# Masks' stage of a graph attention layer: three tiles of sixteen take a mask of outer neighbours from VectorE, and denominators are inverted in a dense form reached by transfers

## What is computed

```
# x is layer-normed
seq = (x @ W_seq).reshape(N, H, DH)                     # N=2048, H=16, DH=32
score1, score2 = einsum('nhd,d->hn', seq, a1), einsum('nhd,d->hn', seq, a2)
scores = leaky_relu(score1[:, :, None] + score2[:, None, :], 0.2)
scores = scores + (1.0 - adj)[None, :, :] * MASK_VAL    # adj is 0 or 1
attn = softmax(scores, axis=-1)
hidden = einsum('hij,jhd->ihd', attn, seq)
```

## Time and profile before

| | us |
|---|---|
| median of three runs | 2346.68 (2344.52 to 2347.96) |
| the profiled execution | 2353.32 |
| its span | 2351.6 |
| masks' stage, first mask to last multiplication | 124.7 to 736.1 |
| PE, DVE, ACT busy over the span | 2117.2, 1557.5, 1090.1 |

### The profile page before, as it was taken

The page is one execution under the profiler, slowest core; times in us unless marked ns, Lnnn a source line. Parts: engine busy times, 40 slices in busy tenths (PEclk is TensorE's granted clock), DMA queues, the critical chain, the costliest instruction groups (busy, mean ns, idle before and its releaser), DMA issues. The chain is left out here.

```text
span 2351.6 us, 43031 instructions
## 1 busy us (share of the span) xinstructions
PE 2117.2 (90%) x18260; PEld 1238.6 (53%) x18260; DVE 1557.5 (66%) x2507; ACT 1090.1 (46%) x1071; POOL 552.0 (23%) x413
## 2 busy tenths in 40 slices
PE   6799999999996899969999998999992599999997
PEld 3444444444443344434444444444461488888886
DVE  7768888888885766747777778776336544444442
ACT  5667888888882233313344444444431222222221
POOL 0000000000001112333454555545521222222211
PEclk9899999999998999958999999999976699999999
DMA  7421211212114111353113031011030444444431
GB/s 253 142 62 42 72 52 62 75 39 76 49 47 156 64 50 72 136 124 76 29 28 82 19 80 29 23 37 46 23 135 36 152 117 117 117 117 113 113 66 23
DMA packets 81711, 185.27 MB, mean 79 GB/s; under 512 B 8785, under 2 KB 18001, under 8 KB 75985
## 3 DMA queue, kind: packets, MB, share of 16 engines
q1 hardware_dynamic: 72560, 161.56, 21.0%
q0 software_dynamic: 8960, 20.98, 4.8%
HBM read 137.81 MB, written 40.37 MB: 76 GB/s over the span
## 5 line engine op out<-in xcount | busy, mean ns | idle before, releaser
L450 ACT ACTIVATE m_step<-m_ub,gat_bias 128x2048 bf16<-128x2048 f32 x256 | 494.3, 1994 | 119.7 <-DVE m_mask L527 106.2
L1266 DVE TENSOR_REDUCE t_rm<-t_m 128x1 f32<-128x512 f32 (+3 forms) x640 | 373.2, 606 | 167.9 <-PE t_m L1374 98.2
L1196 ACT ACTIVATE t_E<-t_s 128x1024 f32<-128x1024 f32 (+3 forms) x320 | 277.7, 896 | 426.9 <-PE t_s L1391 224.8
L527 DVE TENSOR_TENSOR m_mask<-m_step,gat_adjT 128x2048 bf16<-128x2048 bf16 x256 | 306.8, 1222 | 84.8 <-ACT m_step L450 72.8
L1143 POOL TENSOR_TENSOR t_total<-t_E 128x1024 f32<-128x1024 f32 (+2 forms) x160 | 308.1, 1938 | 209.5 <-PE t_d L1418 204.5
L567 PE MATMUL m_bd<-m_mask,m_S 128*32 128x512 bf16 x3072 | 211.9, 380 | 8.1 <-DVE m_mask L527 7.8
L567 PE MATMUL m_bd<-gat_adjT,m_S 128*32 128x512 bf16 x3072 | 211.8, 380 | 4.9 <-PE m_dn L567 4.9
L567 PE MATMUL m_bd<-m_mask,m_neg 128*32 128x512 bf16 x3072 | 211.4, 380 | 0.0
L1374 PE MATMUL t_m<-tq_K,tq_Q 96*128 96x512 f32 (+2 forms) x320 | 145.3, 482 | 34.5 <-DVE t_rm L1266 16.5
L1756 POOL DMA_INDIRECT out<-e_ye,e_token x40 | 80.9, 2024 | 350.4 <-DVE e_ye L1858 341.6
L1922 PE MATMUL e_h<-e_xTh,e_w1h 128*128 128x320 f32 x512 | 159.6, 312 | 3.5 <-PE e_y L1941 2.1
(11 more groups left out here) (306 smaller groups left out, 3689.9 us busy)
## 6 DMA issues: line engine op xcount, KB each, us to landing
a_adj<-in_adj SPq DMA_DIRECT2D x16, 1024.0 KB, 4.9
m_ub<-scratch_uac SPq DMA_DIRECT2D x16, 1024.0 KB, 4.7
e_w1r<-in_L_ffn_w SPq DMA_DIRECT2D x8, 2048.0 KB
e_w2r<-in_L_ffn_w SPq DMA_DIRECT2D x8, 2048.0 KB, 8.8
tq_Q<-scratch_parts SPq DMA_DIRECT2D x48, 256.0 KB, 4.8
m_scale<-scratch_uac SPq DMA_DIRECT2D x32, 256.0 KB
scratch_parts<-o_hi SPq DMA_DIRECT2D x32, 256.0 KB, 2.1
scratch_parts<-o_lo SPq DMA_DIRECT2D x32, 256.0 KB, 2.4
```

Of the source, the lines that this page charges most:

```text
L450: act.activation(step[n % RELUS][:, :], ub[h % 2][:, :], ACT.Relu, bias=bias[:, j, h:h + 1], scale=BIG).then_inc(step_ready, 1)
L527: dve.tensor_tensor(mask[n % MASKS][:, :], step[n % RELUS][:, :], adjT[:, j, :], ALU.min).then_inc(mask_ready, 1)
L1196: act.activation(E[n % 3][:, two, off:BANK], ps_s[:, two, off:BANK], ACT.Exp, scale=SCALE).then_inc(exp_done[z], 1)
L1266: dve.tensor_reduce(rm[:, h, t, ch:ch + 1], ps_m[i % 2][:, 0:w], AX, ALU.max).then_inc(entry_read, 1)
```

## The change

In tiles 1, 5 and 9 (`OUTER`) DVE makes a second mask, adjacency minus mask: the neighbours of the lower branch. PE then needs one product with it where it needed two, with `adjT` and with `neg`. It does this one tile later (`outer_products`). The outer masks are kept in parts of other buffers that are free then, two of them, in 16 chunks of 128.

The division changes its form. `near` is no longer loaded in spread form and added by DVE: its row goes into a seventh row of `dsum`, and the matmul adds it up. The matmul gives four rows (one for each quarter of i) instead of 128. DVE copies them to SBUF (`sums`), four transfers lay them out as 128x16 (`dense`), DVE inverts these 16 columns (`inverses`), one transfer stores them in DRAM, another loads them spread to 128 partitions (`rec`, which is `near`'s place), and DVE multiplies. The places in the order change too: `total` behind tile 5, `sums` before 7, `inverses` before 11, `divide` before 15. The last head keeps the old form: a full matmul, and a reciprocal of 128x512.

```diff
-def stage_masks(nc, sem, keep, uac_dram, near_dram):
+OUTER = (1, 5, 9)
+def stage_masks(nc, sem, keep, uac_dram, near_dram, inv_dram):
...
-        rec = dsum
+        rec, dense = near, st.sb("dense", [P, N // P])
...
-        SCALES = 16 * (2 * 5 + 1)
+        SCALES = 16 * (2 * 5)
+        late, used = hT[:, :, 3, :].bitcast(BF16), seq[:, :, 0:P].bitcast(BF16)
+        outer = lambda h, k: (late if h < 4 else used)[:, :, k % 2 * P:(k % 2 + 1) * P]
...
                 def load_scales(h):
                     if h >= 1:
-                        sp.wait_ge(h_ready, h)
+                        sp.wait_ge(taken[(h - 1) % 2], 2 * ((h - 1) // 2 + 1))
...
-                    chunks = near_dram[h, :].rearrange("(c i) -> c i", c=4)
-                    sp.dma_start(near[:, :], chunks[:, None, :].to_broadcast([4, TILE, BANK])).then_inc(scale_in, 16)
+                def near_row(h):
+                    sp.wait_ge(dsum_ready, h + 1)
+                    for c in range(4):
+                        q = TILE * c + 2 * SPLITS
+                        sp.dma_start(dsum[q:q + 1, :], near_dram[h:h + 1, c * BANK:(c + 1) * BANK]).then_inc(near_in, 16)
+
+                def invert(h):
+                    sp.wait_ge(sums_ready, h + 1)
+                    for c in range(4):
+                        sp.dma_start(dense[TILE * c:TILE * (c + 1), :],
+                                     dsum[c:c + 1, :].rearrange("o (p i) -> o p i", p=TILE)).then_inc(dense_in, 16)
+                    sp.wait_ge(inv_ready, h + 1)
+                    sp.dma_start(inv_dram[h, :].rearrange("(p i) -> p i", p=P), dense[:, :]).then_inc(inv_out, 16)
+                    sp.wait_ge(inv_out, 16 * (h + 1))
+                    chunks = inv_dram[h, :].rearrange("(c i) -> c i", c=4)
+                    sp.dma_start(rec[:, :], chunks[:, None, :].to_broadcast([4, TILE, BANK])).then_inc(rec_in, 16)
...
+                        near_row(h - 1)
+                        load_scales(h)
+                        invert(h - 1)
                         store(h - 1)
-                        load_scales(h)
...
+                def sums(h):
+                    dve.wait_ge(db_full, h + 1)
+                    dve.tensor_copy(dsum[0:4, :], db[0:4, :]).then_inc(sums_ready, 1)
+
+                def inverses(h):
+                    dve.wait_ge(dense_in, 64 * (h + 1))
+                    dve.reciprocal(dense[:, :], dense[:, :]).then_inc(inv_ready, 1)
+
                 def divide(h):
-                    dve.wait_ge(db_full, h + 1)
-                    lk(dve.tensor_tensor(rec[:, :], db[:, :], near[:, :], ALU.add))
-                    lk(dve.reciprocal(rec[:, :], rec[:, :]))
+                    if h < H - 1:
+                        dve.wait_ge(rec_in, 16 * (h + 1))
+                    else:
+                        dve.wait_ge(db_full, h + 1)
+                        lk(dve.reciprocal(rec[:, :], db[:, :]))
                     dve.tensor_tensor(U[:, :], U[:, :], rec[:, :], ALU.mult).then_inc(h_ready, 1)
...
+                    if j in OUTER:
+                        k = number(h, j)
+                        dve.wait_ge(mask_ready, n + 1)
+                        if k >= 2:
+                            dve.wait_ge(outer_free, k - 1)
+                        dve.tensor_tensor(outer(h, k), adjT[:, j, :].rearrange("p (t q) -> p t q", t=T),
+                                          mask[n % MASKS][:, :].rearrange("p (t q) -> p t q", t=T),
+                                          ALU.subtract).then_inc(outer_ready, 1)
...
-                        if h >= 1 and j == 9:
+                        if h >= 1 and j == 7:
+                            sums(h - 1)
+                        if h >= 1 and j == 11:
+                            inverses(h - 1)
+                        if h >= 1 and j == 15:
                             divide(h - 1)
...
                 def total(h):
                     pe.wait_ge(dsum_ready, h + 1)
-                    pe.matmul(db[:, :], pick[:, :, :].rearrange("p c d -> p (c d)"), dsum[:, :],
-                              start=True, stop=True).then_inc(db_full, 1)
+                    pe.wait_ge(near_in, 64 * (h + 1))
+                    if h < H - 1:
+                        pe.matmul(db[0:4, :], pick[:, :, 0], dsum[:, :], start=True, stop=True).then_inc(db_full, 1)
...
```

More of the change, by code:

```diff
@@ L371, in stage_masks @@
         GR = SPLITS * H
-        SCALES = 16 * (2 * 5 + 1)
+        SCALES = 16 * (2 * 5)
+        late, used = hT[:, :, 3, :].bitcast(BF16), seq[:, :, 0:P].bitcast(BF16)
+        outer = lambda h, k: (late if h < 4 else used)[:, :, k % 2 * P:(k % 2 + 1) * P]
+        number = lambda h, j: h * len(OUTER) + OUTER.index(j)
+        outer_ready, outer_free = sem("m_outer"), sem("m_outer_free")
+        near_in, sums_ready, dense_in, inv_ready, inv_out, rec_in = (
+            sem("m_" + n) for n in ("near_in", "sums", "dense_in", "inv", "inv_out", "rec_in"))
         with nc.Block() as block:
@@ L388, in _ @@
                     pool.wait_ge(setup, 7 + s)
-                pool.affine_select(out=pick[:, :, :], in_=pick[:, :, :], compare_op=ALU.is_ge, fill=0.0, base=5,
+                pool.affine_select(out=pick[:, :, :], in_=pick[:, :, :], compare_op=ALU.is_ge, fill=0.0, base=2 * SPLITS,
                                    pattern=[[TILE, 4], [0, TILE]], channel_multiplier=-1).then_inc(setup, 1)
@@ L434, in _ @@
                     if h >= 1:
+                        near_row(h - 1)
+                        load_scales(h)
+                        invert(h - 1)
                         store(h - 1)
-                        load_scales(h)
                     if h + 2 < H:
                         load_u(h + 2)
+                near_row(H - 1)
                 store(H - 1)
@@ L570, in total, with outer_products @@
                     pe.wait_ge(dsum_ready, h + 1)
-                    pe.matmul(db[:, :], pick[:, :, :].rearrange("p c d -> p (c d)"), dsum[:, :],
-                              start=True, stop=True).then_inc(db_full, 1)
+                    pe.wait_ge(near_in, 64 * (h + 1))
+                    if h < H - 1:
+                        pe.matmul(db[0:4, :], pick[:, :, 0], dsum[:, :], start=True, stop=True).then_inc(db_full, 1)
+                    else:
+                        pe.matmul(db[:, :], pick[:, :, :].rearrange("p c d -> p (c d)"), dsum[:, :],
+                                  start=True, stop=True).then_inc(db_full, 1)
+                def outer_products(h, j, down):
+                    k = number(h, j)
+                    pe.wait_ge(outer_ready, k + 1)
+                    for s in range(SPLITS):
+                        for c in range(4):
+                            mm = pe.matmul(down[c * TILE:(c + 1) * TILE, :], S[h % 2][:, j, s, DH:2 * DH],
+                                           outer(h, k)[:, 4 * c:4 * c + 4, :], start=False, stop=False)
+                    mm.then_inc(outer_free, 1)
                 pe.wait_ge(setup, 10)
@@ L589, in _ @@
                         first, last = j == 0, j == T - 1
-                        for s in range(SPLITS):
-                            for c in range(4):
-                                spread(down, S[r][:, j, s, DH:2 * DH], adjT[:, j, :], c,
-                                       start=(first and s == 0), stop=False)
+                        if j not in OUTER:
+                            for s in range(SPLITS):
+                                for c in range(4):
+                                    spread(down, S[r][:, j, s, DH:2 * DH], adjT[:, j, :], c,
+                                           start=(first and s == 0), stop=False)
+                        if j - 1 in OUTER:
+                            outer_products(h, j - 1, down)
                         pe.wait_ge(mask_ready, n + 1)
@@ L599, in _ @@
                                        start=(first and s == 0), stop=(last and s == 2))
-                        for s in range(SPLITS):
-                            for c in range(4):
-                                spread(down, neg[r][:, j, s, :], moving, c, start=False, stop=(last and s == 2))
+                        if j not in OUTER:
+                            for s in range(SPLITS):
+                                for c in range(4):
+                                    spread(down, neg[r][:, j, s, :], moving, c, start=False, stop=(last and s == 2))
                         for c in range(4):
@@ L605, in _ @@
                         mm.then_inc(mask_free, 1)
-                        if h >= 1 and j == 4:
+                        if h >= 1 and j == 5:
                             total(h - 1)
@@ L2008, in program @@
                         stage_factors(nc, sem, keep, scratch["uac"])
-                    stage_masks(nc, sem, keep, scratch["uac"], scratch["near"])
+                    stage_masks(nc, sem, keep, scratch["uac"], scratch["near"], scratch["inv"])
                 recycle()
@@ L2020, in program @@
```

(2 more changed lines are left out.)

## The result

The changed kernel takes 2330.12 us (median of 5 runs, 2328.93 to 2332.77) beside 2344.71 us for the kernel before (5 runs, 2341.41 to 2347.96): a ratio of 0.9937, 95% interval 0.9923 to 0.9951. That is 14.6 us faster; predicted were 7.5 us, and 2330 lies under the range. The prediction started from 2346.68, the median of three of these five runs of before; 2.0 us of the distance between 2339.2 and 2330.12 come from that. Repeated later beside other runs of before, the ratio was 0.9950 (0.9923 to 0.9977), 13.7 us.

The account below looks back on a forecast made before the run. It took the ACT and DVE hand-over of two step buffers to bound the head. Start, second head, thirteen heads, last head and last denominators: -0.6 - 1.5 - 6.0 - 2.4 + 3.0 = -7.5, from 2346.7 to 2339.2 us; range 2333 to 2350.

Parts of the forecast that it names:

- What bounds the head: Masks' stage: ACT and DVE, handing over two step buffers, set the 37.00 us head; PE follows with 0.8 to spare.
- The walk: Masks' stage: waiting-rule arithmetic carried out for all 16 steps and masks of a head; the forecast period was 36.54 us.
- the rule of blocks: Other DVE work of length b between masks costs ACT b - 1.25, or b - 1.51 us after a back-to-back mask.
- The prediction's 34.3 for PE: PE's own work per head after the change, in us, with three tiles dropping 12 matmuls each, 1.94 in all.
- Rival (b): Masks' stage: PE really is the bound and its 31 us show, giving 2319; chance 0.05 with anything halfway.
- the denominators' matmul, with four rows of output instead of 128, at the old 1.18: PE behind tile 5: the narrower matmul still takes 1.18 us, so DVE's copy waits 0.18 for it.
- The two ends: Stage's start and end: first head -0.6, second -1.5, last -2.4, last denominators +3.0 us.
- The chain of the inverses: Reciprocal at tile 11 to multiplication at 15: DRAM store and spread load take 7.4 us, hidden within 9.4.
- Rival (d): Before mask 15: inverses come late, each us beyond 9.4 costs one in 14 heads, up to 2361; chance 0.10.
- The outer masks: DVE, three per head: each costs 1.26 us, chunks of 128 in the output taken as free.
- (c): DVE: outer masks cost 0.2 us more each, 6 us in all, so no change, 2345; chance 0.19.
- (e): DVE: outer masks run at one element a cycle, 2.3 us each, period 39.5, time 2385; chance 0.04.

Follow-up runs that it names:

- the two kernels with moved places: Changed kernel with outer masks, denominators' matmul, copy and dense reciprocal at other tiles: 2308.49 us; with a third step buffer also: 2302.0 us.
- The full matmul: Changed kernel with 128 output columns for the denominators' matmul in every head, the whole bank copied: 2336.23 us, ratio 0.9947 to the kernel before.
- With the row there early: Changed kernel, but the last head's outer sums are loaded spread ahead of need and added by DVE: 2330.63 us, ratio 0.9931 to the kernel before.
- the kernel with the inversion alone: Changed kernel with no outer masks, only the dense inversion: 2351.76 us, ratio 1.0020 to the kernel before.

## Why the prediction was right in kind and wrong in size

**What bounds the head: right.** The pair ACT and DVE sets it, not PE. The outer masks alone take PE's work away and make the kernel 1.1% slower; the third step buffer alone, which leaves PE's work as it is, makes the kernel before faster. The walk gave the period within 0.05 us in five kernels: by the rule of blocks 39.3, 37.4 and 36.53, and with three step buffers, where it takes PE's own work as the bound, 36.5 and 34.85. It was 0.4 short in the two kernels with moved places, where PE comes to 39.67 of 40 us. There PE is the bound, and the denominators' matmul is not free: its two passes start 0.43 apart and occupy their own column group for 0.86, and nothing in the head lets that group catch up. The prediction's 34.3 for PE less its 1.18 plus 0.86 gives 33.98, and 34.63 with 12 matmuls more, an estimate; measured are 33.94 and 34.59. Rival (b) is out.

**The failed step: "the denominators' matmul, with four rows of output instead of 128, at the old 1.18".** The prediction had that matmul end 1.18 behind its start, the copy wait 0.18 for it, and PE stand on it. It ends after 1.02 and PE's next groups run beside it. The copy can start 0.14 earlier, and ACT's wait at tile 7 is 2.03 instead of 2.2. The full matmul brings back 36.53 with a wait of 0.17 before the copy and of 2.25 on ACT, so this term alone makes the 0.22 by which the period was off. In the steady heads it is 13 x 0.22 = 2.9 us of the 7.1 that were missing, the largest part that the runs can name.

**The two ends, mis-sized.** The second head gained 1.7 for 1.5, the last 2.6 for 2.4, the first nothing for 0.6. The last denominators cost 1.8 for 3.0. This comes apart in the rows: from the taking to the matmul's start 3.12 us instead of 0.75, +2.4 (the four issues took 0.28 us each, where 0.31 to 0.66 was taken, and PE started 1.3 us behind the last of them, where a landing of 2.1 was taken); the matmul itself 2.04 instead of 1.12, +0.9, which the prediction did not have: PE, idle for the 3.28 us before, ran it at a granted clock of 0.50, the 1.2 GHz level; -0.8, since before the change DVE's own work ran beyond the matmul's end (730.45 to 731.34), which the prediction overlooked; and -0.7 for the addition. With the row there early, all four vanish, and 6.87 is back. The issues of the row (timeline of the SP queue):

```profile
716.14 1.10 SPq L438 DMA_DIRECT2D m_dsum<-scratch_near  x4
```

The part of the clock varies from run to run: the same matmul behind 3.10 us of idleness took 1.51 at a mean granted clock of 0.68 in the repeat, and 1.25 at 0.83 in the kernel with the inversion alone. In the repeat the last denominators therefore cost 1.1. Within the stage the ends make -2.5 where -1.5 was forecast.

**Outside the stage.** Between the medians lie 14.6 us, or 13.7 the second time, and in the stage 11.4 and 11.8 (735.45 to 723.60). The 2 to 3 us that remain have no place that holds: the stretch behind the stage was 2.2 us shorter in one profile of the changed kernel and 0.5 in the other, and the runs of before differ among themselves by more (2341 to 2356). From the start of the last multiplication to the end, the two profiled executions of before took 1617.9 and 1607.2 us, the two of the changed kernel 1604.8 and 1606.5, the ten other kernels 1605.9 to 1615.4; the 1615.4 and one of 1606.4 belong to two kernels that differ in the last head alone. The attention stage of 620.4 us is no mark of before either: the version with three buffers and moved places has one of 620.5. So these 2 to 3 us are not shown to be the change's, and what they are stays open. In the stage the forecast of 7.5 missed 3.9 us, of which 2.9 are the steady heads, 0.2 the second head, 0.2 the last one, 1.2 the last denominators, less 0.6 for the first. The 11.4 us alone, taken from 2346.7, would give 2335.3, inside the range; that 2330 lies under it takes the 3.2 outside the stage and the 2.0 of the starting value as well.

**The chain of the inverses: right.** 7.4 us was taken; 6.1 to 8.1 were measured with the division moved, and 8.8 in the one head of the full matmul. DVE comes to tile 15 8.4 us behind the reciprocal's end (413.15 to 421.57), and no wait shows there in the changed kernel; in the full matmul's one head it is 0.27. So the room is smaller than the 9.4 us after which ACT would pay, and it was only just enough. Both halves move: the writing takes 1.46 to 3.54 us, the load 4.6 to 5.2 where 2.7 + 2.1 was reckoned. Rival (d)'s price is real: two tiles earlier, the kernel is 1.7% slower than before, in one run.

**The outer masks: right.** L575 takes 1224 to 1227 ns in all 48 cases, each of them in 16 chunks of 128, and the plain mask (L568) 1224 in the median; rivals (c) and (e) are out. The Trainium skill, "VectorE: DVE Perf Modes", section "The perf-mode tier table", has 1224 for it, and the trace agrees for the chunked output also.

**The waits foretold.** ACT's are in the rows (1.89, 2.03, 1.27, 0.36 for 1.9, 2.2, 1.3, 0.4). PE's at tiles 3, 7 and 11 are there, but add up to 1.82 (0.32 + 0.70 + 0.80) for 2.2, mostly as the first was reckoned at 0.5. DVE's 0.2 before the copy is not there, and from the last dsum to its matmul it was 3.12 for about 3.5.

## What to carry to other kernels

Where two engines hand each other a few buffers, write down what a block of other work on one costs the other, and check it on the head as it is; it then gives the gain of an edit that no engine's busy share shows, and says which edits pay only together. When a matmul gets narrower, don't carry its old place on TensorE over: what runs beside it counts, when its reader gets the result, and whether its own column group can catch up before the head ends. A chain on which everything waits at the end should be taken out of the loop's code and kept in the form that starts earliest.

## What the runs showed of the hardware

- A matmul with 4 output columns in fp32 (402.17, two passes of 0.59) ran together with matmuls of 32 columns at other places of the array (402.18); the one with 128 columns did not (403.71, next 404.77). The Trainium skill, "TensorE: Matmul & The Clock Gate", section "Part 3: Packing small matmuls — row/col tiling", describes matmuls of 32 columns at different places that run at the same time; that a fp32 matmul of 4 columns between bf16 ones does it too is what these rows add.
- Writing 128 x 64 bytes to DRAM and being told took 1.46 to 1.49 us in 90 of 150 heads, in the ten traces with the dense inversion, and up to 3.54 in the rest, a spread that one row of a trace doesn't show.
- PE's granted clock was 0.50 for a matmul behind 3.28 us of idleness, and 1.00 for the same matmul behind 0.90; 2.04 and 1.12 us. Behind 3.1 to 3.3 us of idleness it took from 1.25 to 2.04 us in eight traces, so one trace doesn't tell this cost.
- One execution of a kernel had an attention stage of 620.4 us and another of 610.9, with the same program.
